# A recurrent layer's rotations and centring moved to VectorE, which reads them out of PSUM

## What is computed

```
u = jnp.einsum('btd,edh->ebth', x, W_in) + b_in[:, None, None, :]
in_r, in_i, o = (u[0], u[1], u[2])
p = jnp.exp(params_log)
nu, theta, gamma = (p[0], p[1], p[2])
lam = jnp.exp(jax.lax.complex(-nu, theta))
uc = jax.lax.complex(gamma * in_r, gamma * in_i)
...
_, h = jax.lax.associative_scan(combine, (f, uc), axis=1)
...
out = out2[0] - out2[1] + o
y = jax.nn.gelu(out @ w1_w + w1_b, approximate=False)
y = y @ w2_w + w2_b + out
mean = jnp.mean(y, axis=-1, keepdims=True)
var = jnp.var(y, axis=-1, keepdims=True)
y = (y - mean) * jax.lax.rsqrt(var + LN_EPS) * ln_g + ln_b
```

## Time and profile before

| what | value |
|---|---|
| median of 3 runs | 1529.7 us (1526.95 to 1532.33) |
| the profiled execution's own time | 1530.73 us |
| its span in the profile | 1529.0 us |
| busy: PE, DVE, ACT, POOL | 83%, 77%, 73%, 68% |
| recurrent layer with its opening | 0 to about 296 us, the first fifth |

### The profile page before, as it was taken

The page is one execution under the profiler, slowest core; times in us unless marked ns, Lnnn a source line. Parts: engine busy times, 40 slices in busy tenths (PEclk is TensorE's granted clock), DMA queues, the critical chain, the costliest instruction groups (busy, mean ns, idle before and its releaser), DMA issues.

```text
span 1529.0 us, 32894 instructions
## 1 busy us (share of the span) xinstructions
PE 1276.4 (83%) x10332; PEld 782.4 (51%) x10332; DVE 1179.4 (77%) x2871; ACT 1122.6 (73%) x2453; POOL 1032.6 (68%) x1169
## 2 busy tenths in 40 slices
PE   5879998877666678999999999999999999777765
PEld 2435444444343444555566566665666557344433
DVE  7989888369999957776767667776677663699997
ACT  3424342577777749997988988888888895788885
POOL 3477886338888837776767667676676772188887
PEclk9989999979989889999999999999999999899997
DMA  6000000000000000000000000000000000000000
GB/s 193 30 1 1 0 0 0 1 1 0 0 0 0 0 1 2 2 2 2 2 2 2 2 2 2 2 2 1 2 2 2 2 2 1 0 14 27 14 27 27
DMA packets 26242, 14.32 MB, mean 9 GB/s; under 512 B 14406, under 2 KB 25868, under 8 KB 26124
## 3 DMA queue, kind: packets, MB, share of 16 engines
q1 hardware_dynamic: 26124, 12.74, 3.1%
HBM read 8.47 MB, written 4.19 MB: 8 GB/s over the span
## 4 chain that ended last, share of the span: by engine, by line
PE 38%; DVE 20%; issue 18%; POOL 11%; ACT 11%; DVEq 2%; ACTq 0%; DMA 0%; SPq 0%; POOLq 0%
POOL arena L673 5%; PE banks L1734 5%; PE banks L1746 4%; PE banks L1748 4%; DVE arena L1292 4%; DVE arena L1287 4%; PE banks L1673 4%; PE banks L1696 3%; ACT arena L1007 3%; DVE arena L1194 3%; PE banks L1763 3%; PE banks L1765 2%; PE banks L1764 2%; ACT arena L1015 2%; PE banks L1624 2%
## 5 line engine op out<-in xcount | busy, mean ns | idle before, releaser
L673 POOL TENSOR_TENSOR arena<-arena 128x512 f16<-128x512 f32 x384 | 440.4, 1163 | 206.0 <-ACT arena L1015 203.6
L1007 ACT ACTIVATE arena<-banks 128x512 f32<-128x512 f32 x512 | 304.1, 599 | 82.8 <-PE banks L1748 77.6
L1015 ACT ACTIVATE arena<-arena 128x512 f16<-128x512 f32 x512 | 316.1, 631 | 0.1
L1397 DVE TENSOR_REDUCE arena<-banks 128x1 f32<-128x1024 f32 x256 | 309.5, 1216 | 4.4 <-PE banks L1734 2.0
L1763 PE MATMUL banks<-arena 128*128 128x65 f16 x2048 | 213.9, 195 | 12.9 <-POOL arena L673 12.9
L1763 PEld LDWEIGHTS banks<-arena 128*128 128x128 f16 x2048 | 190.1, 97 | 50.4 <-issue 23.1
L1414 DVE TENSOR_TENSOR arena<-arena 128x512 f16<-128x512 f32 x128 | 102.1, 798 | 147.5 <-ACT arena L1015 147.5
L1764 PE MATMUL banks<-arena 128*128 128x64 f16 x2048 | 214.1, 192 | 0.0
L1765 PE MATMUL banks<-arena 128*128 128x65 f16 x2048 | 213.3, 193 | 0.0
L1292 DVE MATCH_REPLACE8 arena<-arena 128x256 f32<-128x256 f32 x512 | 205.1, 407 | 0.4 <-issue 0.4
L1287 DVE MAX8 arena<-arena 128x8 f32<-128x256 f32 x512 | 189.9, 411 | 17.8 <-ACT arena L850 13.1
(11 more groups left out here) (203 smaller groups left out, 2819.9 us busy)
## 6 DMA issues: line engine op xcount, KB each, us to landing
x<-in_L_attn_a_x SPq DMA_DIRECT2D x8, 512.0 KB, 3.9
out<-x SPq DMA_DIRECT2D x8, 512.0 KB, 2.9
arena<-arena SPq DMA_DIRECT2D x64, 1.0 KB, 1.9
arena<-in_L_attn_a_W_in SPq DMA_DIRECT2D x1, 768.0 KB, 5.9
arena<-in_L_attn_a_W_mid SPq DMA_DIRECT2D x1, 512.0 KB, 6.8
arena<-in_L_attn_a_w_w SPq DMA_DIRECT2D x2, 256.0 KB, 6.9
arena<-in_L_attn_b_Wq SPq DMA_DIRECT2D x1, 512.0 KB
arena<-in_L_attn_b_Wo SPq DMA_DIRECT2D x1, 512.0 KB
```

The source lines that it names most:

```text
L673: nc.gpsimd.tensor_tensor(pr_lo[c][:, kt, :], pr[:, kt, :], pr_hi[c][:, kt, :], ALU.subtract).then_inc(a_lP, 1)
L1007: nc.scalar.activation(pr[:, kt, :], ps[6 + kt % 2][:, :], ACT.Exp, scale=SM_SCALE).then_inc(a_P, 1)
L1015: nc.scalar.activation(pr_hi[c][:, kt, :], pr[:, kt, :], ACT.Copy).then_inc(a_hi, 1)
L1397: nc.vector.tensor_reduce(mx[c][:, j:j + 1], psum[:, 2 * pair:2 * pair + 2, :].rearrange("p a b -> p (a b)"), X, ALU.max).then_inc(a_mx, 1)
```

## The change

- Gamma goes into the weights: `gam` (one more broadcast load, in the list `small`) is exponentiated on ACT, and POOL multiplies it into the first two matrices of `win`. `win` gets a semaphore of its own and PE's `lru_u(0)` waits for the product.
- ACT's `lru_u` and POOL's `products_in` go. DVE's new `turned_in` reads the banks of `lru_u` itself: per product q two operations (bank + bias) x table of 128x512, eight per chunk, into `turned`. `sums` adds them into `v`. Products q = 0, 1 of chunk n+2 are read ahead of the turning back of chunk n+1, q = 2, 3 behind it.
- `turned_back` on POOL is one product at a time, the first ahead of `rstd2`, the second behind.
- `gain` goes. DVE's new `centred` reads banks 6 and 7: (y - mean) x ln_g, four of 128x256, right behind `stats2`. ACT's `lru_yhat` then only scales `yhat` in SBUF. `rstd2` has two operations instead of four.
- Chunks 0 and 1 use four banks for `lru_u` (2, 3, 6, 7). The 16 weight products on PE go through two banks instead of four, and `lru_u(1)` comes behind them.
- `decT` is filled on POOL, `wmid` is negated on ACT. `bias_rows` and `conv` go from the opening into the ends of DVE's steps 4, 5 and 6.

```diff
@@ banks of lru_u
+        def u_bank(n, q):
+            return 2 + q % 2 + (4 if n < 2 and q > 1 else 0)
@@ POOL, opening
             rstd(0, 0)
+            pool.wait_ge(s_win, 16)
+            pool.wait_ge(s_gam, 1)
+            scaled = win[:, 0:2, :, :].rearrange("p e k h -> p (e k) h")
+            nc.gpsimd.tensor_tensor(scaled, scaled, gam.unsqueeze(1).to_broadcast([P, 2 * KB2, D]),
+                                    ALU.mult).then_inc(s_scaled, 1)
+            pool.wait_ge(s_act0, 2)
+            nc.gpsimd.memset(decT, 0.0).then_inc(s_decay, 1)
+            pool.wait_ge(s_decay, 1)
+            for k in range(KB2):
+                nc.gpsimd.tensor_scalar(decT[:, k, :], decT[:, k, :], decay[:, k:k + 1], 0.0,
+                                        ALU.add, ALU.add).then_inc(s_decay, 1)
             rstd(1, 1)
...
@@ POOL, step
                 if ahead1:
-                    products_in(n + 1, 1 - c)
+                    turned_back(n + 1, 0)
                 if behind:
                     rstd2(n - 1)
                 if ahead1:
-                    products_out(n + 1)
+                    turned_back(n + 1, 1)
@@ DVE
+            def turned_in(n, qs):
+                wait_from(dve, l_dve, (n - 1) * L_STEPS + 2)
+                for q in qs:
+                    e, m = q // 2, q % 2
+                    dve.wait_ge(l_ups, n * 4 + q + 1)
+                    for part, table in enumerate((cosT, sinT)):
+                        nc.vector.scalar_tensor_tensor(out=turned[e][part][:, m, :], in0=ps[u_bank(n, q)][:, :],
+                                                       scalar=gbias[:, q:q + 1], in1=table[:, m, :],
+                                                       op0=ALU.add, op1=ALU.mult).then_inc(l_u, 1)
...
+            def centred(n):
+                wait_from(dve, l_x, n)
+                dve.wait_ge(l_st2, n * 8 + 8)
...
+                for j in range(TPC):
+                    nc.vector.scalar_tensor_tensor(out=yhat[:, j, :],
+                                                   in0=ps[6 + j // 2][:, D * (j % 2):D * (j % 2) + D],
+                                                   scalar=ymv[:, j, 0:1], in1=lng,
+                                                   op0=ALU.subtract, op1=ALU.mult).then_inc(l_yc, 1)
@@ DVE, step
                 if ahead1:
-                    turned_in(n + 1, 1 - c)
+                    sums(n + 1)
+                    scan(n + 1, 1 - c, 0)
                 if behind:
                     stats2(n - 1)
+                    centred(n - 1)
                 if ahead1:
-                    scans(n + 1, 1 - c)
-                if behind:
-                    gain(n - 1)
+                    scan(n + 1, 1 - c, 1)
+                if ahead2:
+                    turned_in(n + 2, (0, 1))
+                if ahead1:
+                    turned_back(n + 1, 1 - c)
+                if ahead2:
+                    turned_in(n + 2, (2, 3))
@@ ACT
             def lru_yhat(n):
-                act.wait_ge(l_r2, n * 4 + 4)
...
+                act.wait_ge(l_r2, n * 2 + 2)
                 for j in range(TPC):
+                    act.wait_ge(l_yc, n * TPC + j + 1)
+                    nc.scalar.activation(yhat[:, j, :], yhat[:, j, :], ACT.Copy,
                                          scale=yrs[:, j:j + 1]).then_inc(l_y, 1)
```

More of the change, by code:

```diff
@@ L137, in hybrid_block_kernel @@
         lnb = carve([D])
+        gam = carve([D])
         sinT = carve([KB2, CH])
         decT = carve([KB2, CH])
-        u = [[carve([KB2, CH]) for _ in range(2)] for _ in range(2)]
+        turned = [[carve([KB2, CH]) for _ in range(2)] for _ in range(2)]
         pa, pb = carve([KB2, CH]), carve([KB2, CH])
@@ L498, in rstd, with turned_back @@
                                         rs[:, bass.ds(of * TPC, TPC), 0], ALU.mult).then_inc(ln_p, 1)
[L501 to L512, removed]
+            def turned_back(n, part):
+                pool.wait_ge(l_dve, n * L_STEPS + 4)
+                nc.gpsimd.tensor_tensor((pa, pb)[part], g[0], (cosT, sinT)[part], ALU.mult).then_inc(l_pool, 1)
             def add_ln_bias(n):
@@ L762, in _ @@
             lru_z(0, 0)
-            lru_u(0, 0, range(4))
             lru_z(1, 1)
-            lru_u(1, 1, range(4))
+            act.wait_ge(s_w2, N_W2)
+            nc.scalar.activation(wmid[:, 1, :, :], wmid[:, 1, :, :], ACT.Copy, scale=-1.0).then_inc(s_par, 1)
             def put(n, dsts, cols):
                 act.wait_ge(s_pe0, n + 1)
-                src = ps[4 + n % 4][:, 0:cols]
+                src = ps[4 + n % 2][:, 0:cols]
                 if len(dsts[0].shape) == 3:
@@ L1164, in _ @@
                 m *= 2
-            link(nc.vector.memset(decT, 0.0))
-            for k in range(KB2):
-                link(nc.vector.tensor_scalar(decT[:, k, :], decT[:, k, :], decay[:, k:k + 1], None, ALU.add))
             dve.sem_inc(s_dve0, 1)
-            def turned_in(n, c):
-                ur, ui = u[c]
-                base = n * 12
-                dve.wait_ge(l_u, n * 4 + 4)
-                if not (isinstance(n, int) and n == 0):
-                    dve.wait_ge(l_dve, base)
-                nc.vector.tensor_tensor(ta, ui, sinT, ALU.mult).then_inc(l_dve, 1)
-                nc.vector.tensor_tensor(tb, ur, sinT, ALU.mult).then_inc(l_dve, 1)
@@ new lines, in sums, with scan @@
+            def sums(n):
+                dve.wait_ge(l_u, n * 8 + 8)
+                wait_from(dve, l_dve, n * L_STEPS)
+                nc.vector.tensor_tensor(v[0], turned[0][0], turned[1][1], ALU.add).then_inc(l_dve, 1)
+                nc.vector.tensor_tensor(v[1], turned[1][0], turned[0][1], ALU.subtract).then_inc(l_dve, 1)
+            def scan(n, c, e):
+                base = n * L_STEPS
+                dve.wait_ge(l_dve, base + 1 + e)
+                for k in range(KB2):
+                    first = 0.0 if c == 0 else h[0][e][:, k, CH - 1:CH]
+                    nc.vector.tensor_tensor_scan(g[e][:, k, :], decT[:, k, :], v[e][:, k, :], first,
+                                                 ALU.mult, ALU.add).then_inc(l_dve, 1)
@@ L1523, in _ @@
             transposes(0, zrow, 0)
-            pe.wait_ge(s_w2, N_W2)
+            pe.wait_ge(s_scaled, 1)
             lru_u(0, 0, range(4))
             transposes(1, zrow, 0)
-            lru_u(1, 1, range(4))
+            pe.wait_ge(s_w2, N_W2)
             pe.wait_ge(s_w, N_W)
@@ L1563, in _ @@
                     last.then_inc(s_pe0, 1)
+            lru_u(1, 1, range(4))
             pe.wait_ge(s_ev0, 16)
```

139 lines of the change are left out of this document (65 added, 74 removed).

## The result

The changed kernel takes 1519.8 us (median of 9 runs, 1515.17 to 1527.12) against 1529.8 (9 runs, 1526.95 to 1533.06): ratio 0.994, 95% interval 0.9918 to 0.9962. The prediction was 1518, with 1505 to 1528 as its range and 0.82 for faster. The profiled execution took 1519.80 us, its span is 1518.0. Busy totals of the two kernels lie close together: VectorE 1179.4 and 1180.1, TensorE 1276.4 and 1277.7, ScalarE 1122.6 and 1098.7, GpSimd 1032.6 and 990.0. VectorE and TensorE have as much work as before, ScalarE and GpSimd 24 and 43 us less; what shrank is the time in which VectorE and TensorE wait.

The account below looks back on a forecast made before the run. The prediction took VectorE, with GpSimd, to set the pace and TensorE to be close behind. Opening and step savings came to 11.5 to 12 us: 1530.73 - 12.0 = 1518.7 profiled, 1518 for the median, range 1505 to 1528.

Parts of the forecast that it names:

- The step pitch: Full steps 2 and 3: 28.4 us against 29.93, VectorE with GpSimd setting the pace, TensorE idling 1.7.
- The 5.4 of collisions: Full step: VectorE waits on GpSimd, 1.7 and 1.4 from the start of sums, 0.3 after centred, 2.0 among imaginary scans.
- Bank operations: VectorE operations reading PSUM: 0.61 us for 512 elements, 0.35 for 256, not held by GpSimd.
- The opening: Before step 0: gam costs 1.2, GpSimd's products 3.9, table ends near 35, step 0 starts at 62.8 instead of 69.18.
- The rivals of dear and of excluding bank operations: VectorE bank operations at 1.13 us, total 1547, chance 0.04; or excluding GpSimd too, total 1531, chance 0.05.
- the second rival: Opening: gam late by 2.1 and lru_u(1) late, 4 to 7 us lost, total 1524; chance 0.18.
- The setup rows: bias_rows and conv: 10.2 us in the opening before, 6.7 once moved into later steps.
- The centring: Full step: centred priced at 4 x 0.35 = 1.4 us on VectorE; gain going saves 1.14 where no later stage waits.
- The first rival: Collisions rarer and TensorE the bound: steps 1 to 5 go down to 26.73, total 1507; chance 0.17.
- Step 1: No next_rstd, but rstd beside sums: 28.9 us against 30.06.
- Step 6: Scans end at 6.0, power of rstd2 at 9.3, emptyings 4.3 more: w1(6) at 245.2 against 256.69.
- Steps 4 and 5: Bias rows add 2.1 and 2.8, ln_stats goes: 30.3 against 29.96 and 29.35 against 28.11.

Follow-up runs that it names:

- e_no_bias: Changed kernel with turned_in's eight bank operations as plain tensor_tensor, bank x table, leaving out the bias gamma b_in: 1516.39 us, ratio 0.9916.
- e_gam_after_sin: Changed kernel with gam still loaded sixth but on its own semaphore, its exponential behind the sine on ScalarE: 1512.84 us, ratio 0.989.
- e_rows_opening: Changed kernel with bias_rows and conv back in the opening, behind turned_in(1) and ahead of step 0: 1519.0 us, ratio 0.9936.
- e_rstd2_four: Changed kernel with the two dropped small rstd2 operations back on GpSimd, results unused, ScalarE waiting for all four: 1530.55 us, ratio 1.0009.
- e_yhat_back: Changed kernel with the centring undone: ScalarE normalises from banks, rstd2 has four operations, VectorE multiplies by ln_g once: 1530.12 us, ratio 1.0019.
- e_lnb_early: Changed kernel with add_ln_bias ahead of rstd in GpSimd's step, right behind residual: 1516.24 us, ratio 0.9925.

## Why the prediction was right, step by step

- **Total and direction.** 12 us forecast in the layer, 12.4 measured there, 11.0 in the span. The median came out 10.0 under the kernel before. Right, but partly for reasons other than those written down, and partly by luck. Step 0 started 1.7 late, steps 0 and 1 took 0.7 and 1.9 more than forecast, together 4.3; steps 2 to 5 took 0.2, 0.4, 1.0 and 1.5 less, together 3.2. So step 6 starts only 1.1 late.
- **The step pitch.** 28.4 forecast, 28.18 and 27.99 measured; TensorE idle ahead of w1 1.0 to 1.2, forecast 1.7; w1 at +15.85, forecast +15.4. Here the forecast added VectorE's work and collisions up to a full engine. The trace has it busy 25.80 of 28.18 (step 2) and idle for 2.4, of which 2.05 are waits for `lru_u`. The prediction did see that q = 3 came at 22.4 "just when `turned_in` comes to q = 2", and stopped there: this equality was the loop. The 5.4 of collisions were about 2.2 on VectorE (busy 25.8, less 23.0 and 0.6 for dearer bank operations), of which 1.8 are L1182; the second product fell behind the imaginary scans, as L516 at 159.23 shows. And w1's time was worked out along VectorE, `centred` at 10.8 and the power at 11.1 behind it; the trace has the power end at 11.8, behind GpSimd's own queue.
- **Bank operations.** Forecast 0.61 and 0.35, measured 0.66 and 0.395 (1.66 for four). The Trainium skill's formula (VectorE: DVE Perf Modes, section on the errata) had given 0.66, so for this form it was nearer than my row. For the plain form `e_no_bias` has 0.60, as the earlier trace rows said: the 0.06 goes with the form (one scalar operand and one operation more on each element; the two are not told apart). The term was mis-sized by 0.6 us a step (8 x 0.05 and 4 x 0.045). Without the 0.06 of the eight the steps are 0.1 to 0.3 shorter in `e_no_bias`, since VectorE idled beside them. That bank operations are not held by GpSimd was right: 64 of them lie between 721 and 752 ns. The rivals of dear and of excluding bank operations fell.
- **The opening.** Step 0 at 64.50, forecast 62.8. The failing term is `gam`: 1.2 taken, bound 2.1, and the first exponential came 2.5 later (7.70 against 5.19). `e_gam_after_sin` gives 1.83 back. That is the first half of the second rival. The decay operations cost 1.09; the gamma product held one doubling operation for 2.00 (L1157 at 14.81) and `add_ln_bias(0)` another for 2.08 (L1159 at 30.93). The table ended at 35.9, forecast 35. The lateness of `lru_u(1)`, its second half, never showed: nothing waited for it. The two held operations in the trace of the changed kernel:

```profile
14.81 2.00 DVE L1157 SCALAR_TENSOR_TENSOR arena<-arena 128x1 f32<-128x1 f32 x1
...
30.93 2.08 DVE L1159 SCALAR_TENSOR_TENSOR arena<-arena 128x128 f32<-128x128 f32 x1
```

- **The setup rows.** The sum credited their move with 10.2 less 6.7, that is 3.5. Undone it changes w1(6) by 4.4 and the layer's end by 1.8, with the clock of w1(6) between the two; alone it is worth 2.5 at the end (294.49 against 296.94). The 10 us at the start of step 0 were real. Alone, they went back in two held operations of step 0 and in steps 4 and 5.
- **The centring.** Credited with nothing but `gain`, and `rstd2`'s two lost operations with nothing at all. That is the step which failed: undone alone it takes 10.3 us (1530.12 and 1519.8), and the two operations by themselves take 10.8 (1530.55 and 1519.8). The forecast's number held because the collisions that it counted too high (5.4, measured about 2.2) stood in for the loop it did not count (2.4 of idle time and the dearer bank operations). That was luck.
- **The first rival** (TensorE the bound) was wrong for the full steps of this kernel, though step 5 is one (TensorE busy 27.87 of 27.87). Its pitch was reached by moving one GpSimd operation: 26.8 to 27.0 in steps 1 to 3. Its total, 1507, was not: 1516.24.
- **Step 1** was forecast at 28.9 and took 30.80, because w1(1) ran at a low clock (6.75 at a granted clock of 0.54); in the executions with 27.64 to 27.75 it took 3.71, and that is the difference. The clock in one execution was no term of the sum.
- **Step 6.** w1(6) 12.27 after `sums`, forecast 13.7; start 232.62, forecast 231.5; together 244.89 against 245.2.
- **Steps 4 and 5** took 29.26 and 27.87, forecast 30.3 and 29.35. Without the bias rows, in `e_rows_opening`, they take 2.0 and 1.6 less: the 2.1 was right, the 2.8 too high by 1.2. In step 5 TensorE is the bound. Where the other 1.0 of step 4 went stays open.

## What to carry to other kernels

When two engines both look 90% full and each shows a wait for the other, don't add up either of them: follow one item around the loop, from the start of one step to the start of the next, and price the edit by what it does to that path. Follow the engine that is not full too: here GpSimd, idle for over a third of the step, carried 11.8 us of the loop's 28.0. Two four-element operations on it were worth ten microseconds, part of them by the clock, and eight long operations a step made cheaper beside the loop were worth almost none. An edit undone alone and the same edit made alone are two different experiments: the centring measured ten one way and nothing the other.

## What the runs showed of the hardware

- A wait ahead of TensorE can cost more than its length. With 1.0 to 1.2 us of idle time ahead of it w1 took 3.71 in steps 2 to 4 of the changed kernel; with 2.4 to 2.7 it took 5.2 to 5.4 in five of the six such steps of `e_rstd2_four` and `e_yhat_back`, with part of w1 at a granted clock of 0.50 (1.2 GHz). The idle time alone doesn't decide. It took 5.40 after 1.91 in step 3 of `e_rows_opening`, and 3.71 after 2.66 in step 4 of `e_yhat_back`, after 3.41 in step 1 of `e_gam_after_sin` and after 2.80 in step 3 of the kernel before, whose step 4 had 5.32 after 2.85. What decides between these stays open.
- VectorE's `scalar_tensor_tensor` with a per-partition scalar takes 0.06 us more than the plain `tensor_tensor`, from a bank, at 512 elements (742 and 681 ns).
- GpSimd's operations on four elements took 0.19 us beside bank operations (L528 in `e_rstd2_four`, 161.00) and 1.1 to 1.2 beside a scan or a VectorE operation with two SBUF inputs (1.14 for L529 beside it, 1.18 for L546 in the earlier trace rows); its power took 1.01 beside `centred` (`e_lnb_early`, 150.74) and 1.84 to 1.95 beside scans.
